# Scoring the second head of each pair from 16-bit halves in a fused attention and feed-forward kernel

## The reference

```python
x = x + 0.5 * ffn(layernorm(x), W_up, W_gate, W_down)      # weights made ternary
x = x + attn(layernorm(x), Wq, Wk, Wv, Wo, head_scale)     # 16 heads, 4 KV heads of 128, rotary, causal
x = x + 0.5 * ffn(layernorm(x), W_up, W_gate, W_down)

q, k = apply_rotary(x @ Wq), apply_rotary(x @ Wk)          # t * cos + rotate_half(t) * sin
scores = einsum('bhid,bhjd->bhij', q, k) / sqrt(128)       # causal mask
out = einsum('bhij,bhjd->bhid', softmax(scores), v) * head_scale
```

## Time and profile before

| | |
|---|---|
| median of 3 runs | 1135.9 us (1135.78 to 1137.19) |
| profiled execution, its own time | 1136.0 us |
| its span, first to last instruction | 1134.2 us |
| granted clock of TensorE, mean | 0.989 of full speed |
| busy share PE / DVE / ACT / POOL | 95% / 85% / 70% / 63% |
| attention | from about 228 to 950 us |

### The profile page before, as it was taken

The page is one execution under the profiler, slowest core; times in us unless marked ns, Lnnn a source line. Parts: engine busy times, 40 slices in busy tenths (PEclk is TensorE's granted clock), DMA queues, the critical chain, the costliest instruction groups (busy, mean ns, idle before and its releaser), DMA issues.

```text
span 1134.2 us, 27100 instructions
## 1 busy us (share of the span) xinstructions
PE 1073.0 (95%) x8465; PEld 839.6 (74%) x8465; DVE 959.3 (85%) x2369; ACT 790.2 (70%) x1964; POOL 719.0 (63%) x886
## 2 busy tenths in 40 slices
PE   4697888979999999999999999999999998999998
PEld 2354555658888888888888888888888886555555
DVE  5787888699999999999999999999999997433433
ACT  4363665568878888878878788788787885554453
POOL 4653555567777777777777777777777773544443
PEclk9798999999999999999999999999999999999999
DMA  9421112134533443434344434334344344100101
GB/s 347 116 48 38 38 37 55 20 60 76 80 71 71 82 76 70 80 71 89 66 77 83 79 69 79 74 74 79 69 79 79 69 79 80 29 20 18 37 18 37
DMA packets 262130, 79.88 MB, mean 70 GB/s; under 512 B 249296, under 2 KB 260816, under 8 KB 261840
## 3 DMA queue, kind: packets, MB, share of 16 engines
q1 hardware_dynamic: 261664, 79.19, 33.8%
q10 hardware_dynamic: 432, 0.27, 0.1%
HBM read 12.85 MB, written 4.19 MB: 15 GB/s over the span
## 4 chain that ended last, share of the span: by engine, by line
PE 70%; issue 10%; POOL 8%; DVE 7%; ACT 3%; DMA 1%; DVEq 0%; POOLq 0%; ACTq 0%
PE bank L666 45%; PE bank L727 14%; POOL SCR L386 6%; PE bank L655 4%; PE bank L627 3%; PE bank L637 3%; DVE X L853 1%; DVE SCR L863 1%; ACT SCR L557 1%; DMA SCR<-ARENA 1%; ACT SCR L473 1%; DVE SCR L827 1%; DVE ARENA L1032 1%; ACT NHL L465 1%; POOL RSTD L373 1%
## 5 line engine op out<-in xcount | busy, mean ns | idle before, releaser
L414 POOL TENSOR_SCALAR SCR<-SCR,RI 128x128 f32<-128x128 f32 (+1 forms) x512 | 309.3, 604 | 44.0 <-DVE RI L1028 3.8
L399 POOL TENSOR_TENSOR SCR<-SCR 128x512 f32<-128x512 f32 x160 | 203.2, 1270 | 150.2 <-DVE SCR L993 148.9
L557 ACT ACTIVATE SCR<-bank,NM 128x128 f32<-128x128 f32 (+1 forms) x512 | 208.5, 419 | 125.4 <-DVE NM L1012 125.4
L386 POOL TENSOR_TENSOR SCR<-SCR 128x512 f16<-128x512 f32 x128 | 154.2, 1205 | 196.4 <-ACT SCR L479 196.2
L863 DVE SCALAR_TENSOR_TENSOR SCR<-SCR,CS,bank 128x512 f32<-128x512 f32 x128 | 95.3, 745 | 128.7 <-PE bank L637 90.4
L727 PE MATMUL bank<-SCR 128*128 128x128 f32 (+1 forms) x1024 | 193.2, 331 | 3.7 <-ACT SCR L557 3.7
L529 ACT COPY SCR<-bank 64x512 f32<-64x512 f32 x320 | 185.7, 580 | 13.8 <-PE bank L666 7.3
L1032 DVE TENSOR_TENSOR ARENA<-SCR,ARENA 128x768 f16<-128x768 f32 x128 | 187.8, 1467 | 4.3 <-ACT ARENA L564 3.4
L666 PE MATMUL bank<-WOH,ARENA 128*128 128x256 f16 x1024 | 188.5, 273 | 2.2 <-DVE ARENA L1023 1.3
L479 ACT CAST SCR<-SCR 128x512 f16<-128x512 f32 x128 | 79.1, 618 | 152.8 <-DVE SCR L863 102.9
L1012 DVE CUSTOM_DVE_ANT_0 bank<-bank,MASK,SCQ 128x128 f32<-128x128 f32 (+1 forms) x512 | 182.9, 417 | 0.8
(11 more groups left out here) (113 smaller groups left out, 1646.7 us busy)
## 6 DMA issues: line engine op xcount, KB each, us to landing
out<-X SPq DMA_DIRECT2D x7, 512.0 KB, 2.9
X<-in_x SPq DMA_DIRECT2D x1, 2560.0 KB, 10.4
ARENA<-in_wq SPq DMA_DIRECT2D x1, 2048.0 KB, 12.9
ARENA<-in_wo SPq DMA_DIRECT2D x1, 2048.0 KB, 18.1
SCR<-ARENA SPq DMA_TRANSPOSE x128, 3.6
X<-in_x SPq DMA_DIRECT2D x3, 512.0 KB, 9.6
X<-in_wu SPq DMA_DIRECT2D x1, 1024.0 KB, 6.8
X<-in_wg SPq DMA_DIRECT2D x1, 1024.0 KB, 9.0
```

Source lines behind the costliest of these rows:

```text
L386: gp.tensor_tensor(HL[:, f % 4, :], H32[:, f % 2, :], HH[:, f % 4, :], ALU.subtract).then_inc(s["hl_done"], 1)
L399: gp.tensor_tensor(dst, M1[:, m, :], M2[:, m, :], ALU.add).then_inc(add, 1)
L414: last = gp.tensor_scalar(EX[:, par, lo:hi], EX[:, par, lo:hi], RI[:, par, c:c + 1], PS, ALU.mult, ALU.mult)
L557: last = act.activation(EX[:, par, 384 * hh + lo:384 * hh + hi], SBK[hh][:, lo:hi], ACT.Exp, bias=NM[:, par, c:c + 1], scale=-1.0, accum_o ...
```

## The change

The first head of a pair is scored as before. For the second head, ACT makes a 16-bit high half of the rotated q (`QH`, 256 columns of `QF`) in every step, and POOL the low half `QL` = `QF` - `QH`. For K, at `k` = 0, ACT makes `KH` of all 512 columns and POOL `KL`. PE then makes the second head's scores with the helper `pairs`, in three products: high by high, high by low, low by high. ACT's copies stand at the end of its step, and wait for POOL's rope add; POOL's subtractions stand after the normalisation and wait for ACT's copies; PE waits for the low halves ahead of the second head. `QH` and `QL` lie in a part of `SCR` that attention doesn't use otherwise; `KH` and `KL` are new tensors.

```diff
+        QH, QL = pieces(2048, 2304, F16, 2), pieces(2304, 2560, F16, 2)
+        KH, KL = (sb(n, [P, 2, 512], F16) for n in ("KH", "KL"))
...
+            def rope_lo(r, full, hi, lo):
+                gp.wait_ge(qk_hi, r + 1)
+                gp.tensor_tensor(lo, full, hi, ALU.subtract).then_inc(qk_lo, 1)
...
                     if real(b, i, 2):
                         norm(t - 2, i % 2)
+                    if real(b, i, 0):
+                        if k == 0:
+                            rope_lo(r - 1, KF[:, g, :], KH[:, g, :], KL[:, g, :])
+                        rope_lo(r, QF[:, i % 2, SEQ:], QH[:, i % 2, :], QL[:, i % 2, :])
                     if i == 0 and ends(b) is not None:
                         rows_rstd(ends(b))
...
                     if i == 2 and ends(b) is not None:
                         rows_hi(ends(b))
+                    if real(b, i, 0):
+                        if k == 0:
+                            act.wait_ge(add, r)
+                            wait(act, s_done, 8 * u - 8)
+                            act.copy(KH[:, g, :], KF[:, g, :]).then_inc(qk_hi, 1)
+                        act.wait_ge(add, r + 1)
+                        wait(act, s_done, 2 * t - 2)
+                        act.copy(QH[:, i % 2, :], QF[:, i % 2, SEQ:]).then_inc(qk_hi, 1)
...
                 for hh in range(2):
+                    if hh == 1:
+                        pe.wait_ge(qk_lo, 5 * u + i % 4 + 2)
                     wait(pe, ex, 2 * t + hh - 1)
                     bk = SBK[hh]
                     for blk, (lo, hi) in enumerate(BLOCKS):
-                        last = pe.matmul(bk[:, lo:hi], QF[:, i % 2, hh * SEQ + blk * P:hh * SEQ + (blk + 1) * P],
-                                         KF[:, g, kv * SEQ:kv * SEQ + hi - lo], start=blk == 0, stop=blk == 1,
-                                         skip_group_check=True)
+                        if hh == 0:
+                            last = pe.matmul(bk[:, lo:hi], QF[:, i % 2, blk * P:(blk + 1) * P], KF[:, g, kv * SEQ:kv * SEQ + hi - lo],
+                                             start=blk == 0, stop=blk == 1, skip_group_check=True)
+                        else:
+                            q = [a[:, i % 2, blk * P:(blk + 1) * P] for a in (QH, QL)]
+                            k = [a[:, g, kv * SEQ:kv * SEQ + hi - lo] for a in (KH, KL)]
+                            last = pairs(bk[:, lo:hi], lambda c: q[0], lambda c: q[1], lambda c: k[0], lambda c: k[1], 1, blk == 0, blk == 1)
                     last.then_inc(s_done, 1)
```

More of the change, by code:

```diff
@@ L175, in program @@
         half_done, out_done = sem("last_sums_half_done"), sem("out_done")
-        proj, swap, mul, add, v_hi, v_lo = (
-            sem(n) for n in ("proj_done", "rope_swapped", "rope_mul", "rope_add", "v_hi", "v_lo"))
+        proj, swap, mul, add, qk_hi, qk_lo, v_hi, v_lo = (
+            sem(n) for n in ("proj_done", "rope_swapped", "rope_mul", "rope_add", "qk_hi", "qk_lo", "v_hi", "v_lo"))
         s_done, mx, ex, rcp, pn = (
```

## The result

The changed kernel takes 1218.3 us, median of 4 runs (1217.43 to 1219.25), against 1136.08 us beside it: 1.072 times as long, 95% interval 1.070 to 1.074. The forecast was 1218, range 1188 to 1251. The total was met almost to the microsecond; how it is made up was not, as the experiments show.

What follows compares the result with a forecast made beforehand. The prediction took DVE, full and tied with PE, to bound attention, with POOL's new subtractions colliding with it. 1136.0 + 72 (Q's collisions) + 10 (K's subtractions) = 1218 us, range 1188 to 1251.

Steps and rivals of the forecast that it cites:

- DVE is full, PE's gain can't be cashed: Attention: PE saves 0.16 us a step, 21 us in all, but DVE's room lets at most 3.3 us count.
- DVE and POOL exclude each other: DVE operations with two SBUF operands and POOL instructions reading SBUF shut each other out, instruction by instruction.
- 0.57 us in each of 126 steps, 72 us: Q's subtraction on POOL, put at 0.73 us, collides with DVE's SIN multiplication; steps go from 4.73 to 5.30 us.
- They meet, every middle step: POOL's subtraction would start at 617.24 and DVE's next SIN at 617.26, so they collide in each middle step.
- K's subtractions a quarter visible, 10 us: 32 subtractions of 1.28 us in each unit's first step; between 0 and 41 us shows, a quarter taken.
- ACT's copies at nothing, bounds 0 and 26 us: The copy ahead of the next swap just fits ACT's idle time; cost nothing, bounds 0 and 0.2 us a step.
- The 0.43 ns an element: Rate for ACT's copies, from 618 ns for 512 elements and 840 for 768; about 0.4 us for 256.
- PE's wait for the low halves at nothing: PE wants the low halves two steps later, after POOL's subtraction has ended, so its wait costs nothing.
- The margin of 1.0 us: PE's second-head scores at 619.0 come 1.0 us behind the end of POOL's subtraction.
- The sum: 1136.0 plus 72 for Q's collisions plus 10 for K's subtractions, copies and PE's wait at nothing: 1218 us.
- the even sum: Every middle step grows by 0.57 us, and K's subtractions carry 10 of 82 us.
- the signs named: POOL above 85% busy, its SIN wait nearly gone, longer SIN or L1032, pace 5.2 to 5.4 us, PE visibly waiting.

Runs made afterwards that it cites:

- the products alone: Changed kernel without ACT's copies and POOL's subtractions; second head scored in three 16-bit products with weight halves as operands: 1136.9 us, ratio 0.9999.
- the memset runs: Changed kernel with memsets of about equal length replacing all subtractions: 1170.9 us; or with K's subtraction dropped and only Q's replaced by a memset: 1143.4 us.
- the one for Q alone: Changed kernel without K's subtraction and with Q's replaced by a memset of about the same length, same waits and signals: 1143.4 us, ratio 1.007.
- the run with Q's alone: Changed kernel without POOL's subtraction for K, Q's kept; K's high half stands in for its low one: 1169.9 us, ratio 1.029.
- the run with SIN first: Changed kernel with ACT's copies behind the next swap, K's subtraction halved over two steps, and DVE multiplying by SIN before COS: 1214.4 us, ratio 1.068.

## Why the prediction was right, and where it was not

- **DVE is full, PE's gain can't be cashed.** Right, and more strictly than said: allowed were 3 us, the products alone gave 0 (ratio 0.999 to 1.001). The reading that decided was that DVE appears in no row of the waits, while PE's share of 100% and the chain of waits pointed to PE.
- **DVE and POOL exclude each other, and POOL's read makes it so.** Right. It is the largest single cause: 47 of the 82 us vanish when POOL's instruction only writes, and in part of the rest the late rope add collides. The Trainium skill ("SBUF — State Buffer", SBUF: two separate sides) says that a DVE operation with two SBUF inputs is shut out only by a GpSimd one that reads SBUF; the memset runs agree: with the one for Q alone the middle steps are at 4.73 and SIN at 0.68. Its wording that the loser fully blocks agrees in kind; the rows give 0.52 to 0.54 us for a rest of 0.66 to 0.68 (the 1.20 of the step above, K's 1.70 below).
- **0.57 us in each of 126 steps, 72 us.** The mechanism was right, its size and number wrong. Where it stands alone it is 0.40: the subtraction takes 0.67, not 0.73, and the next POOL instruction starts with it nearly ended (632.20 against 631.03 + 1.20). And it stands at only four places of a batch (both K, and Q2 and Q3 of the second unit, 0.37 to 0.40 each). I had drawn up one step and multiplied it by 126. Where DVE has the last layer's rows to prepare besides, at Q1 and Q2 of the first unit (5.7 and 5.6 us already before), the subtraction is over before SIN comes. In the run with Q's alone:

```profile
606.72 0.67 POOL L406 TENSOR_TENSOR SCR<-SCR 128x256 f16<-128x256 f32 x1
```
```profile
607.81 0.69 DVE L1016 TENSOR_TENSOR SCR<-SCR,SIN 128x512 f32<-128x512 f32 x1
```

  Q's term is 26 us, not 72. "They meet, every middle step" was read from one step.
- **K's subtractions a quarter visible, 10 us.** Wrong, by the step that POOL waits longest there and so most of it hides. Alone they cost 27 us, and with Q's 21 more. The chain is one that I had looked at and priced at nothing: behind the copy on ACT's queue lie the swap and the exponentials. After K's subtraction and Q's the rope add of the next step is late, ACT's copy waits for it, the swap behind the copy is late, DVE idles. In the changed kernel, POOL, ACT and DVE in turn:

```profile
607.11 1.70 POOL L406 TENSOR_TENSOR KL<-SCR,KH 128x512 f16<-128x512 f32 x1
608.77 1.44 POOL L406 TENSOR_TENSOR SCR<-SCR 128x256 f16<-128x256 f32 x1
610.18 1.26 POOL L402 TENSOR_TENSOR SCR<-SCR 128x512 f32<-128x512 f32 x1
...
613.53 0.67 POOL L406 TENSOR_TENSOR SCR<-SCR 128x256 f16<-128x256 f32 x1
```
```profile
611.56 0.40 ACT L594 CAST SCR<-SCR 128x256 f16<-128x256 f32 x1 [2.37 <-POOL SCR L402]
611.99 1.17 ACT L540 COPY SCR<-bank 64x512 f32<-64x512 f32 x2
```
```profile
607.12 0.67 DVE L1018 TENSOR_TENSOR SCR<-SCR,SIN 128x512 f32<-128x512 f32 x1
...
608.73 0.96 DVE L1057 TENSOR_TENSOR ARENA<-SCR,ARENA 128x768 f16<-128x768 f32 x1 [0.25 <-ACT ARENA L575]
...
613.19 0.69 DVE L1018 TENSOR_TENSOR SCR<-bank,COS 128x512 f32<-128x512 f32 x1 [1.28 <-ACT SCR L540]
613.80 0.95 DVE L1018 TENSOR_TENSOR SCR<-SCR,SIN 128x512 f32<-128x512 f32 x1
```

  SIN stretches K's subtraction by 0.54 us (1.70 instead of 1.16), and L1057 then Q's by 0.77 (1.44 instead of 0.67): the two collisions in a row are 1.3 us of the lateness. The add ends at 611.44, ACT has waited 2.37 us, DVE 1.28. The step has 6.68 us instead of 4.72. Taking the copy out from in front of the swap gives 17 us back, splitting K's subtraction over two steps gives 12.
- **ACT's copies at nothing, bounds 0 and 26 us.** 7 us, within the bounds. Missed was the start of the second unit, where two swaps follow the copy. The 0.43 ns an element in the working is a slip: 840 - 618 over 256 elements is 0.87 ns. The 0.4 us for 256 fits that, and 0.41 was measured.
- **PE's wait for the low halves at nothing.** About 5 us. The margin of 1.0 us held in most steps; once in a unit, behind K's and Q's subtractions, PE's matmuls wait up to 1.9 us.
- **The sum.** 72 + 10 + 0 + 0 against 26 (Q) + 27 (K) + 21 (where they meet) + 7 (copies) + 0 (products) = 81. That both give 82 is partly chance: Q's term was 46 us too high, K's with the meeting 38 too low, the copies' 7 too low. The range held by the same luck: both of its ends are the even sum, with other lengths of the subtraction (and, at the low end, nothing for K and 4 us off). With the measured length of 0.667 the even sum would have given, as an estimate, 1136 + 126 x 0.51 + 10 = 1210. Of the signs named, POOL busy was to be above 85% and is 423 of 500, 84.6%; its wait for SIN was to be nearly gone and still has 43.5 of 103.9 us; the pace of 5.2 to 5.4 us in every step is not there, but 4.7 and 6.7 in turn.

## What to carry to other kernels

When the busiest engine by the chain is tied with another, ask which of them never waits: the wait list answers that, and an edit to the other one gives nothing. POOL's idle share is free room for an instruction that only writes (Q's memset cost nothing), but not for one that reads SBUF while DVE works with two SBUF operands (26 us for the same place). Look at the places of the instructions, and at which of them a delay pushes onto each other: the sum of lengths alone missed here (the run with SIN first). And price a new operation at every kind of step of the loop, not at the middle one times the count: what decides is the step where it meets the rarest other work, and what is queued behind its wait.

## What the runs showed of the hardware

- A memset of POOL held up no DVE operation with two SBUF operands (SIN 0.68 us from 595.53 beside a memset from 595.51), a subtraction of nearly the same length does: 27 against 75 us in this kernel at the same places.
- When a POOL and a DVE instruction that exclude each other start nearly together, either can win. SIN did at recorded starts of 631.02 against 631.03, and also where the subtraction's start was recorded first (607.11 against SIN's 607.12); the subtraction did where it was 0.27 us ahead (613.53 against 613.80, SIN 0.95 us). So starts 0.01 us apart don't tell the winner, the lengths do. The loser's length in the profile contains its wait, so POOL's 1.20 or DVE's 0.95 is no duration of the work.
- POOL's subtraction of 16-bit out of float32 takes 0.667 us for 256 elements and 1.155 for 512, so 1.9 ns an element and 0.18 us fixed: the fixed part is smaller than that of its one-operand instructions (0.26).
